# A macaron block on one core: attention without its loop, chunk pairs merged onto the front chunk, keys in twelve pieces, values in quarters

## The chip, the cores and the metric

The kernel runs on one core of one Trainium2 chip, as one program. The metric is the device time in microseconds, and less is better. The engines are named as in the profile: PE (TensorE, matmuls), PEld (its weight loads), DVE (VectorE), ACT (ScalarE), POOL (GpSimd) and SP (SyncE, which here only issues DMAs).

## The reference, cut to what matters

```
x = x + 0.5 * ffn(layernorm(x))          # routed FFN: 128 picked tokens of 1024
x = x + attn(layernorm(x))               # the part that is changed
x = x + 0.5 * ffn(layernorm(x))

# attn: x is (8, 2048, 256): 8 batches, 2048 tokens, 8 heads of 32
q, k, v = lowrank(xh, Uq, Vq, bq), lowrank(xh, Uk, Vk, bk), lowrank(xh, Uv, Vv, bv)
scores = einsum('bqhd,bkhd->bhqk', q, k) / 32 ** 0.5
out = einsum('bhqk,bkhd->bqhd', softmax(scores), v)
```

All of it is float32. The attention takes in for every batch and head a matrix of 2048 x 2048 probabilities.

## The kernel before, in words

The stages follow one another: the first FFN, `project` (q, k and v into HBM as `qk_parts` and `v_tokens`), `attend`, the second FFN. Only `attend` is changed. It has five instruction streams, one for each engine, which are written out by hand and meet in semaphores.

**Units.** A batch has two groups of four heads (`g`), and a group four blocks of 512 queries (`u`), so it has 8 units `un` = 0 to 7, and the stage has 64. A unit has 16 chunks `c` of 128 keys. A chunk gives four tiles, one a head: PE computes the scores into one of three PSUM banks of `at_ps_s` (L1774), ACT takes their exponentials into `at_probs` (L1653), and PE multiplies them by the values into `at_ps_acc` (L1721, `pv`, signalled as `pv_done`). A cycle of a unit is one chunk: four scores, the `pv` of the chunk before, and four matmuls into `at_ps_max` (L1687), by which PE is working out the row maxima of a later unit; DVE reduces these (L1538, L1540) and ACT copies a part (L1602). The maxima reach the queries over a small DMA pair on SP (`row_of_max`, L1408), for which PE waits at the start of each unit (`max_in`, L1791).

**The softmax sums.** `at_probs` is a ring of 8 chunks: chunk c + 8 of the stream reuses the slot of chunk c. POOL sums the chunks 0 to 13 into `at_pool_sum`, in seven additions of 128x2048 (L1516), which I number 0 to 6. It gets help: for the six pairs (2,3), (4,5) ... (12,13) of `DMA_PAIRS` an accumulating DMA of 1 MB, issued by POOL (L1493, `start_pair`), adds one chunk onto the other, and I number these 0 to 5. Addition n, for n over 0, waits until transfer n - 1 has landed. Transfers 0 and 1 are issued ahead of addition 1, and transfer n ahead of addition n from there on (`DMA_BEFORE_ADD`). Chunks 14 and 15 are summed by PE. In cycle 5 of the next unit PE closes the sums (`close_z`, L1732 and L1736), for which it waits for addition 6. Before the exponentials of a chunk ACT waits in `free(c)` for whoever still reads its slot: POOL's addition, the transfer, or the close.

**Loads.** SP issues in each unit, in this order: eight loads of queries for the unit three ahead; a piece of the next group's keys or values; the store of the unit before's result (L1417, once DVE has it); another piece; the `row_of_max` pair, once ACT has the row; in some units a third piece. Keys are loaded in the units with u = 0 to 2 and values (`load_v`, L1392, two halves of 512 KB) in those with u = 3. At the start of each unit with u = 0 PE waits for the values of its group (L1790). All of SP's loads and stores go through one queue, POOL's transfers through another.

**The loop.** Batches 0 and 7 are written out, and 1 to 6 are a loop of three passes of two batches on each engine.

Of the kernel before, what the change touches and what calls it, by code (L numbers as in the profile page):

```python
# [15 lines left out]
P = 128  # L16
# [4 lines left out]
ALU = mybir.AluOpType  # L21
# [3 lines left out]
B, S, D = 8, 2048, 256  # L25
T = S // P
H, DH = 8, 32
HG = P // DH
NG = H // HG
# [1206 lines left out]
DMA_PAIRS = ((2, 3), (4, 5), (6, 7), (8, 9), (10, 11), (12, 13))  # L1236
DMA_BEFORE_ADD = (1, 1, 2, 3, 4, 5)
POOL_CHUNKS = (0, 1, 3, 5, 7, 9, 11, 13)
CLOSE_IN = 5
NORM_IN = 6  # L1240
TURN_MAX_IN = 13
RINGS = 3


def score_banks(tiles, per_cyc):

    users = [w for j in range(tiles) for w in ((j, "m") if j == TURN_MAX_IN * per_cyc + 1 else (j,))]
    order, last, laps = list(range(RINGS)), {}, []  # L1250
    for lap in range(3):
        bank, after = {}, {}
        for w in users:
            if w == CLOSE_IN * per_cyc + 2:
                after["z"] = last.get(RINGS - 1)
                last[RINGS - 1] = ("z", lap)
                order = [1, 0]
            if w == (NORM_IN + 1) * per_cyc + 2:
                order.insert(1, RINGS - 1)
            k = order.pop(0)  # L1260
            order.append(k)
            bank[w], after[w], last[k] = k, last.get(k), (w, lap)
        laps.append((bank, {w: (x[0], lap - x[1]) for w, x in after.items() if x}))
    assert laps[1] == laps[2] and laps[0][0] == laps[1][0]
    return laps[1]


def attend(nc, tag, qk, v_dram, out):

    UQ = 512  # L1270
    NU = S // UQ
# [10 lines left out]
    K_LO_ROWS = ((2 * DH, 0, 2), (DH, 2, 4))  # L1282
    LOADS = 8 * 16
    RING = 8
    NQB = 4
    PER_CYC = TILES // NCYC
    SCALE = float(DH) ** -0.5

    dma_sources = [a for a, _ in DMA_PAIRS]
    pool_chunks = list(POOL_CHUNKS)  # L1290
# [9 lines left out]
    with ExitStack() as ctx:  # L1300
# [67 lines left out]
        def _(sp):  # L1368
# [14 lines left out]

            K_PIECES = [(part, *piece) for part, rows in ((0, HI_ROWS), (0, Q_LO_ROWS), (1, K_LO_ROWS)) for piece in rows]

# [5 lines left out]

            def load_v(b, g, half):  # L1392
                first = half * NC // 2
                sp.dma_start(v[:, g, first:first + NC // 2],
                             v_dram[bass.ds(b * S + first * P, S // 2), g * P:(g + 1) * P]
                             .rearrange("(c p) d -> p c d", p=P)).then_inc(v_in[g], 16)

            def load_kv(b, g):
                load_k(b, g, K_PIECES)
                load_v(b, g, 0)  # L1400
                load_v(b, g, 1)

# [24 lines left out]
            def batch(b, first_batch=False, last=False):  # L1427

                for un in range(BU):
                    unit = b * BU + un  # L1430
                    if un + 3 < BU or not last:

                        sp.wait_ge(scores, unit * TILES)
                        sp.sem_inc(load_turn, 1)
                        load_q(b + (un + 3) // BU, (un + 3) % BU)
                    ahead = not first_batch if un < NU else not last
                    to_load = (b if un < NU else b + 1, 1 if un < NU else 0)
                    u = un % NU
                    if u == 0 and ahead:

                        sp.wait_ge(pv_done, unit * NC)
                        sp.sem_inc(load_turn, 1)
                    if u < NU - 1 and ahead:
                        load_k(*to_load, K_PIECES[3 * u:3 * u + 1])
                    elif ahead:
                        load_v(*to_load, 0)
                    if un > 0:
                        store(unit - 1, b, un - 1)
                    elif not first_batch:
                        store(unit - 1, b - 1, BU - 1)  # L1450
                    if u < NU - 1 and ahead:
                        load_k(*to_load, K_PIECES[3 * u + 1:3 * u + 2])
                    elif ahead:
                        load_v(*to_load, 1)
                    if un + 1 < BU or not last:
                        row_of_max(unit + 1, un + 1)
                    if u < NU - 2 and ahead:
                        load_k(*to_load, K_PIECES[3 * u + 2:3 * u + 3])
                if last:
                    store(b * BU + BU - 1, b, BU - 1)  # L1460

            batch(0, first_batch=True)
            with sp.Fori(0, B // 2 - 1) as pair:
                batch(pair * 2 + 1)
                batch(pair * 2 + 2)
            batch(B - 1, last=True)
# [5 lines left out]
        def _(pool):  # L1472
# [11 lines left out]
            def batch(b, first_batch=False):  # L1484
                for un in range(BU):
# [3 lines left out]
                    def start_pair(d):  # L1489
                        a, c = DMA_PAIRS[d]  # L1490
                        pool.wait_ge(pv_done, unit * NC + c + 1)
                        pool.sem_inc(dma_turn, 1)
                        nc.gpsimd.dma_start(probs[:, c % RING], probs[:, a % RING], accum_op=ALU.add  # L1493
                                            ).then_inc(dma_added[(un * ND + d) % 2], 16)

                    for n in range(ADDS):
# [3 lines left out]
                        c = pool_chunks[n + 1]  # L1500
                        paired = [d for d in range(ND) if DMA_PAIRS[d][1] == c]
                        if paired:
# [15 lines left out]
            batch(0, first_batch=True)  # L1518
            with pool.Fori(0, B // 2 - 1) as pair:
                batch(pair * 2 + 1)  # L1520
                batch(pair * 2 + 2)
            batch(B - 1)
# [3 lines left out]
        def _(dve):  # L1526
# [61 lines left out]
            batch(0, first_batch=True)  # L1588
            with dve.Fori(0, B // 2 - 1) as pair:
                batch(pair * 2 + 1)  # L1590
                batch(pair * 2 + 2)
            batch(B - 1, last=True)
# [3 lines left out]
        def _(act):  # L1596
# [72 lines left out]
            batch(0, first_batch=True)  # L1669
            with act.Fori(0, B // 2 - 1) as pair:  # L1670
                batch(pair * 2 + 1)
                batch(pair * 2 + 2)
            batch(B - 1, last=True)
# [3 lines left out]
        def _(pe):  # L1677
# [18 lines left out]
            pe.wait_ge(q_in[0], LOADS)  # L1696
            pe.wait_ge(k_in[0], LOADS)
            for n in range(FOURS):
# [9 lines left out]
            def batch(b, first_batch=False, last=False):  # L1708
                for un in range(BU):
# [67 lines left out]
                    def max_four(n):  # L1777
# [5 lines left out]
                        if n == 0:  # L1783
                            pe.wait_ge(q_in[ahead % NQB], (b * (BU // NQB) + ahead // NQB + 1) * LOADS)
                            if ahead % NU == 0:
                                pe.wait_ge(k_in[ahead // NU % NG], (b + ahead // BU + 1) * LOADS)
# [34 lines left out]
            batch(0, first_batch=True)  # L1821
            with pe.Fori(0, B // 2 - 1) as pair:
                batch(pair * 2 + 1)
                batch(pair * 2 + 2)
            batch(B - 1, last=True)
# [57 lines left out]
```

## Time and the profile before

| | |
|---|---|
| median of 3 runs | 4640.27 us (4639.2 to 4641.36) |
| profiled execution, its own time | 4629.35 us |
| its span | 4627.6 us |
| granted TensorE clock, mean | 0.929 |
| share of the span busy | PE 81%, DVE 71%, ACT 69%, POOL 55% |

The profiled execution is 10.92 us under the median of the timed runs. A span is the time from the first to the last instruction. Idle time of an engine is put down to what released it, so that `<-POOL at_pool_sum L1516` reads as a wait that ended when that addition ended.

### The profile page before, as it was taken

How to read it: one execution, taken by the hardware profiler on the slowest of the kernel's cores; microseconds unless marked ns; L12 is line 12 of the kernel's file. 1: busy time of each engine (PE TensorE's matmuls, PEld its weight loads, DVE VectorE, ACT ScalarE, POOL GpSimd, SP SyncE). 2: the span in 40 equal slices, each digit the busy share in tenths (PEclk: the TensorE clock that was granted, in tenths of full speed). 3: DMA queues.
4: the chain of work that ended last, by engine and by line, in shares of the span. 5: the costliest groups of instructions: out<-in, count | busy, mean ns of one | idle time of the engine just before them, and what ended most of it. 6: DMA issues, size and time to landing. Idle time of an engine off the chain costs nothing. (4 is left out here: it accounts for less than half of the span.)

```text
span 4627.6 us, 72033 instructions
## 1 busy us (share of the span) xinstructions
PE 3742.8 (81%) x21202; PEld 1462.9 (32%) x21202; DVE 3268.7 (71%) x4504; ACT 3216.1 (69%) x6587; POOL 2553.0 (55%) x966
## 2 busy tenths in 40 slices
PE   0176576599999999999999999999999999930276
PEld 0143354133333333333333333333333333310143
DVE  8644465777777877777777777778777777648544
ACT  5143365488888888878888887888888888834043
POOL 0011000377777777776777777677767777754111
PEclk9988788699999999999999999999999999965588
DMA  8200599677878878777887888788787877678100
GB/s 273 74 5 5 208 344 336 138 146 167 175 160 170 177 158 178 168 168 157 169 169 162 177 169 169 155 169 176 156 178 167 169 165 167 130 214 305 43 5 5
DMA packets 326047, 743.31 MB, mean 161 GB/s; under 512 B 26060, under 2 KB 209888, under 8 KB 270112
## 3 DMA queue, kind: packets, MB, share of 16 engines
q0 software_dynamic: 57216, 407.92, 44.3%
q1 hardware_dynamic: 234880, 297.04, 21.6%
q10 hardware_dynamic: 33568, 33.69, 2.1%
q8 instruction: 185, 3.03, 0.3%
q14 instruction: 198, 1.62, 0.1%
HBM read 198.90 MB, written 136.48 MB: 72 GB/s over the span
## 5 line engine op out<-in xcount | busy, mean ns | idle before, releaser
L1653 ACT ACTIVATE at_probs<-at_ps_s 128x512 f32<-128x512 f32 x4096 | 2255.7, 613 | 346.1 <-PE at_ps_s L1774 261.1
L1538 DVE TENSOR_REDUCE at_part_max<-at_ps_max 128x3 f32<-128x1536 f32 x1024 | 1801.0, 1759 | 472.3 <-PE at_ps_max L1687 464.2
L1516 POOL TENSOR_TENSOR at_pool_sum<-at_pool_sum,at_probs 128x2048 f32<-128x2048 f32 x384 | 1771.9, 4614 | 624.4 <-DMA at_probs<-at_probs 623.4
L1774 PE MATMUL at_ps_s<-at_qs,at_ks 97*128 97x512 f32 (+1 forms) x4096 | 1532.9, 452 | 41.2 <-ACT at_probs L1653 21.4
L1721 PE MATMUL at_ps_acc<-at_probs,at_v 128*32 128x512 f32 x8192 | 1097.5, 608 | 0.9 <-ACT at_probs L1653 0.9
L1774 PEld LDWEIGHTS at_ps_s<-at_qs,at_ks 97*128 97x128 f32 (+1 forms) x4096 | 629.8, 188 | 1151.2 <-ACT at_probs L1653 823.5
L1540 DVE TENSOR_REDUCE at_part_max<-at_max_copy 128x1 f32<-128x512 f32 x1024 | 691.6, 675 | 0.0
L1602 ACT COPY at_max_copy<-at_ps_max 128x512 f32<-128x512 f32 x1024 | 610.0, 596 | 88.1 <-PE at_ps_max L1687 87.6
L1687 PE MATMUL at_ps_max<-at_ks,at_qs 32*128 32x512 f32 x4096 | 525.9, 501 | 68.5 <-DMA at_ks<-qk_parts 34.8
L1493 POOL DMA_DIRECT2D at_probs<-at_probs x384 | 346.1, 901 | 220.6 <-PE at_ps_acc L1721 213.6
L1687 PEld LDWEIGHTS at_ps_max<-at_ks,at_qs 32*128 32x128 f32 x4096 | 198.1, 183 | 425.3 <-issue 363.9
L1516 POOL TENSOR_TENSOR at_pool_sum<-at_probs 128x2048 f32<-128x2048 f32 x64 | 292.1, 4563 | 63.2 <-ACT at_probs L1653 63.2
L1721 PEld LDWEIGHTS at_ps_acc<-at_probs,at_v 128*32 128x32 f32 x8192 | 161.4, 108 | 347.4 <-ACT at_probs L1653 296.0
L1553 DVE RECIPROCAL at_rz<-at_ps_s 128x16 f32<-128x16 f32 x64 | 16.5, 258 | 330.0 <-PE at_ps_s L1743 330.0
L278 PE MATMUL s_pt<-s_ident,s_sall 128*128 128x128 f32 x2 | 0.9, 446 | 271.4 <-DVE s_sall L222 271.4
L1473 POOL MEMSET at_ones<- 128x128 f32 x1 | 0.2, 206 | 333.4 <-POOLq L62 333.4
L259 ACT ACTIVATE s_y<-s_x,s_small 128x256 f32<-128x256 f32 x256 | 129.2, 587 | 68.7 <-DVE s_small L213 61.3
L1732 PE MATMUL at_ps_s<-at_probs,at_ones 128*32 128x512 f32 x1024 | 126.7, 613 | 44.7 <-ACT at_probs L1653 44.7
L1213 PE MATMUL pr_pqk<-pr_xT,pr_w 128*128 128x512 f32 x256 | 132.7, 667 | 32.5 <-DVE pr_lo L1116 29.7
L1646 ACT COPY at_zT<-at_ps_s 128x512 f32<-128x512 f32 x64 | 37.6, 587 | 171.6 <-PE at_ps_s L1736 171.6
L624 POOL TENSOR_TENSOR f_att<-f_att,f_rowsum 128x1280 f32<-128x1280 f32 x16 | 49.6, 3097 | 182.3 <-DVE f_rowsum L709 182.3
L772 ACT ACTIVATE f_small<-f_small 128x4 f32<-128x4 f32 x4 | 0.8, 204 | 207.0 <-DVE f_small L671 207.0
(195 smaller groups left out, 2723.4 us busy)
## 6 DMA issues: line engine op xcount, KB each, us to landing
at_probs<-at_probs POOLq DMA_DIRECT2D x384, 1024.0 KB, 8.3
qk_parts<-pr_hi SPq DMA_DIRECT2D x32, 1024.0 KB, 6.4
qk_parts<-pr_lo SPq DMA_DIRECT2D x32, 1024.0 KB, 6.1
at_qs<-qk_parts SPq DMA_DIRECT2D x320, 64.0 KB, 6.0
at_ks<-qk_parts SPq DMA_DIRECT2D x80, 256.0 KB
s_x<-in_x SPq DMA_DIRECT2D x16, 1024.0 KB, 8.6
after_ffn<-s_y ACTq DMA_DIRECT2D x16, 1024.0 KB, 6.5
pr_x<-after_ffn SPq DMA_DIRECT2D x8, 2048.0 KB
```

The lines of the kernel that those rows point to most:

```text
L259: last = nc.scalar.activation(yb[:, k, t, :], xb[:, k, t, :], ACT.Identity, scale=sm[:, k, 0, t:t + 1], bias=sm[:, k, 1, t:t + 1])
L1213: nc.tensor.matmul(pqk[:, m, :], w[:, m // NG, m % NG, :], xT[:, n % 2, m % NG, :], start=True, stop=True).then_inc(qk_done, 1)
L1493: nc.gpsimd.dma_start(probs[:, c % RING], probs[:, a % RING], accum_op=ALU.add).then_inc(dma_added[(un * ND + d) % 2], 16)
L1516: nc.gpsimd.tensor_tensor(acc, a, probs[:, c % RING], ALU.add).then_inc(pool_added, 1)
L1538: nc.vector.reduce_max(part_max[:, 0:HG - 1, t, c], ps_max[:, 0:HG - 1], AX.X).then_inc(three_max_done, 1)
L1540: nc.vector.reduce_max(part_max[:, HG - 1:HG, t, c], max_copy[:, n % 2:n % 2 + 1], AX.X).then_inc(part_max_done, 1)
L1602: nc.scalar.copy(max_copy[:, n % 2], ps_max[:, HG - 1]).then_inc(max_copied, 1)
L1653: nc.scalar.activation(probs[:, c % RING, h], ps_s[:, BANK[j]], ACT.Exp, scale=SCALE).then_inc(exp_done, 1)
L1687: last = nc.tensor.matmul(ps_max[:, h], qs[rows, un % NQB, h, t * P:(t + 1) * P], ks[rows, un % BU // NU, h, c * 512:(c + 1) * 512], start ...
L1721: last = nc.tensor.matmul(ps_acc[h * DH:(h + 1) * DH, :], v[:, k // NU, c, h * DH:(h + 1) * DH], probs[:, c % RING, h], start=(c == 0), st ...
L1732: nc.tensor.matmul(ps_close[h * DH:(h + 1) * DH, :], ones[:, 0:DH], probs[:, c % RING, h], start=(c == RAW_CHUNKS[0]), stop=False)
L1774: nc.tensor.matmul(ps_s[:, BANK[j]], ks[rows, g, h, c * P:(c + 1) * P], qs[rows, un % NQB, h, :], start=True, stop=True).then_inc(scores, 1)
```

## The change

Six edits, all in `attend`:

1. On all five engines the loop over pairs of batches is replaced by batches 1 to 6 written out.
2. The merge goes the other way: chunk c is added onto chunk a of a pair (a, c), where a was added onto c. A transfer now waits for `pv_done` of a and the exponentials of c, where it waited for `pv_done` of c. POOL's additions take the even chunks 2, 4 ... 12, where they took 3, 5 ... 13. So the even slots come free with an addition and the odd ones with a transfer.
3. Keys come in 12 pieces of one head and 256 KB, where they came in 8 of one to three heads. By u they are placed as 1 + 2 + 1, 1 + 2 + 1 and 1 + 3 pieces (ahead of the store, behind it, behind `row_of_max`); they were 1 + 1 + 1 of one head, then two of one head and one of three, and then two of two heads.
4. Values come in quarters of 256 KB, placed 1 + 2 + 1 in the unit with u = 3, where the halves were placed 1 + 1 + 0.
5. The banks of `at_ps_s` go round as 0, 2, 1, where they went 0, 1, 2. With it the close follows tile 19 in its bank, where it followed tile 20, and tile 30 is the one that waits for the normalised result, where tile 31 was.
6. The counts that PE waits for are changed accordingly.

```diff
-POOL_CHUNKS = (0, 1, 3, 5, 7, 9, 11, 13)
+POOL_CHUNKS = (0, 1, 2, 4, 6, 8, 10, 12)
...
-    order, last, laps = list(range(RINGS)), {}, []
+    order, last, laps = [0, 2, 1], {}, []
...
-                order = [1, 0]
+                order.remove(RINGS - 1)
             if w == (NORM_IN + 1) * per_cyc + 2:
-                order.insert(1, RINGS - 1)
+                order.insert(0, RINGS - 1)
...
-    dma_sources = [a for a, _ in DMA_PAIRS]
+    dma_sources = [c for _, c in DMA_PAIRS]
...
-            K_PIECES = [(part, *piece) for part, rows in ((0, HI_ROWS), (0, Q_LO_ROWS), (1, K_LO_ROWS)) for piece in rows]
+            K_PIECES = [(part, to, h, h + 1) for part, rows in ((0, HI_ROWS), (0, Q_LO_ROWS), (1, K_LO_ROWS))
+                        for to, first, end in rows for h in range(first, end)]
...
-            def load_v(b, g, half):
-                first = half * NC // 2
-                sp.dma_start(v[:, g, first:first + NC // 2],
-                             v_dram[bass.ds(b * S + first * P, S // 2), g * P:(g + 1) * P]
-                             .rearrange("(c p) d -> p c d", p=P)).then_inc(v_in[g], 16)
+            def load_v(b, g, quarters):
+                for q in quarters:
+                    first = q * NC // 4
+                    sp.dma_start(v[:, g, first:first + NC // 4],
+                                 v_dram[bass.ds(b * S + first * P, S // 4), g * P:(g + 1) * P]
+                                 .rearrange("(c p) d -> p c d", p=P)).then_inc(v_in[g], 16)
...
                     if u < NU - 1 and ahead:
-                        load_k(*to_load, K_PIECES[3 * u:3 * u + 1])
+                        load_k(*to_load, K_PIECES[4 * u:4 * u + 1])
                     elif ahead:
-                        load_v(*to_load, 0)
+                        load_v(*to_load, (0,))
                     if un > 0:
                         store(unit - 1, b, un - 1)
                     elif not first_batch:
                         store(unit - 1, b - 1, BU - 1)
                     if u < NU - 1 and ahead:
-                        load_k(*to_load, K_PIECES[3 * u + 1:3 * u + 2])
+                        load_k(*to_load, K_PIECES[4 * u + 1:4 * u + (4 if u == NU - 2 else 3)])
                     elif ahead:
-                        load_v(*to_load, 1)
+                        load_v(*to_load, (1, 2))
                     if un + 1 < BU or not last:
                         row_of_max(unit + 1, un + 1)
                     if u < NU - 2 and ahead:
-                        load_k(*to_load, K_PIECES[3 * u + 2:3 * u + 3])
+                        load_k(*to_load, K_PIECES[4 * u + 3:4 * u + 4])
+                    elif u == NU - 1 and ahead:
+                        load_v(*to_load, (3,))
...
-            with sp.Fori(0, B // 2 - 1) as pair:
-                batch(pair * 2 + 1)
-                batch(pair * 2 + 2)
+            for b in range(1, B - 1):
+                batch(b)
...
                         a, c = DMA_PAIRS[d]
-                        pool.wait_ge(pv_done, unit * NC + c + 1)
+                        pool.wait_ge(pv_done, unit * NC + a + 1)
+                        pool.wait_ge(exp_done, unit * TILES + c * HG + HG)
                         pool.sem_inc(dma_turn, 1)
-                        nc.gpsimd.dma_start(probs[:, c % RING], probs[:, a % RING], accum_op=ALU.add
+                        nc.gpsimd.dma_start(probs[:, a % RING], probs[:, c % RING], accum_op=ALU.add
...
                     if u == 0:
-                        pe.wait_ge(v_in[g], b * 32 + 32)
+                        pe.wait_ge(v_in[g], b * 64 + 64)
                     pe.wait_ge(max_in, unit * 32 + 32)
```

Below is SP's stream in the last unit of batch 0 (un = 7, u = 3), in which the values for the next batch's first group are loaded; `at_v` is the value tile, `attention` the store, `at_max_row` the `row_of_max` pair. First of before, then of the change:

```order
L1378 DMA at_qs<-qk_parts 32x3x512
L1381 DMA at_qs<-qk_parts 32x2x512 x2
L1394 DMA at_v<-v_tokens 128x8x128
L1417 DMA attention<-at_o 128x4x128
L1394 DMA at_v<-v_tokens 128x8x128
L1408 DMA at_qs<-at_max_row 1x12x128
L1408 DMA at_qs<-at_max_row 1x4x128
```

```order
L1379 DMA at_qs<-qk_parts 32x3x512
L1382 DMA at_qs<-qk_parts 32x2x512 x2
L1397 DMA at_v<-v_tokens 128x4x128
L1419 DMA attention<-at_o 128x4x128
L1397 DMA at_v<-v_tokens 128x4x128 x2
L1410 DMA at_qs<-at_max_row 1x12x128
L1410 DMA at_qs<-at_max_row 1x4x128
L1397 DMA at_v<-v_tokens 128x4x128
```

The last quarter of the values now stands behind the `row_of_max` pair; before, nothing but the next unit's queries did.

The second place is the unit ahead of it on SP (un = 6, u = 2), in which the last keys are loaded. First of before, then of the change:

```order
L1389 DMA at_ks<-qk_parts 32x2x2048
L1417 DMA attention<-at_o 128x4x128
L1389 DMA at_ks<-qk_parts 32x2x2048
L1408 DMA at_qs<-at_max_row 1x12x128
L1408 DMA at_qs<-at_max_row 1x4x128
```

```order
L1391 DMA at_ks<-qk_parts 32x2048
L1419 DMA attention<-at_o 128x4x128
L1391 DMA at_ks<-qk_parts 32x2048 x3
L1410 DMA at_qs<-at_max_row 1x12x128
L1410 DMA at_qs<-at_max_row 1x4x128
```

One head moved from ahead of the store to behind it. The third place is the end of the loop's body on PE, before:

```order
L1774 MATMUL at_ps_s<-at_qs,at_ks 128x512
L1683 REGISTER_ALU
L1687 MATMUL at_ps_max<-at_ks,at_qs 128x512 x4
L1822 REGISTER_ALU
L1822 COMPARE_AND_BRANCH
L1774 MATMUL at_ps_s<-at_qs,at_ks 128x512 x2
```

In the change the end of a batch is as the end of any unit:

```order
L1775 MATMUL at_ps_s<-at_qs,at_ks 128x512 x2
L1688 MATMUL at_ps_max<-at_ks,at_qs 128x512 x4
L1775 MATMUL at_ps_s<-at_qs,at_ks 128x512 x2
L1722 MATMUL at_ps_acc<-at_probs,at_v 32x512 x4
```

The branch and the register instructions are gone.

## Rows read from the trace of the kernel before

**Rows 1.** The page, costliest group: count, busy, mean ns, idle before, releaser.

```profile
L1653 ACT ACTIVATE at_probs<-at_ps_s 128x512 f32<-128x512 f32 x4096 | 2255.7, 613 | 346.1 <-PE at_ps_s L1774 261.1
```

**Rows 2.** ACT's first copy of each unit, a window a row: count, starts.

```profile
L1640 ACT COPY at_oT<-at_ps_acc x60: 586/629/632, 1021.5 to 3987.0; 128x512 f32<-128x512 f32 x60
L1640 ACT COPY at_oT<-at_ps_acc x16: 596/629/630, 1266.8 to 2016.1; 128x512 f32<-128x512 f32 x16
L1640 ACT COPY at_oT<-at_ps_acc x2: 629/630/630, 1518.3 to 1566.7; 128x512 f32<-128x512 f32 x2
L1640 ACT COPY at_oT<-at_ps_acc x2: 629/629/629, 1466.0 to 1518.3; 128x512 f32<-128x512 f32 x2
L1640 ACT COPY at_oT<-at_ps_acc x5: 586/587/629, 2016.1 to 2224.4; 128x512 f32<-128x512 f32 x5
L1640 ACT COPY at_oT<-at_ps_acc x4: 586/608/629, 2826.8 to 2983.0; 128x512 f32<-128x512 f32 x4
```

**Rows 3.** Waits from 1000 to 4000 us: total, times, longest.

```profile
POOL at_pool_sum L1516 <- DMA at_probs<-at_probs: 601.6, 294, 6.0
...
ACT at_probs L1653 <- POOL at_pool_sum L1516: 72.9, 63, 2.4
...
PE at_ps_s L1774 <- DMA at_qs<-at_max_row: 3.2, 4, 1.5
```

**Rows 4.** POOL's timeline over one unit: start, length, engine, line, idle before.

```profile
1575.81 4.58 POOL L1516 TENSOR_TENSOR at_pool_sum<-at_pool_sum,at_probs 128x2048 f32<-128x2048 f32 x1 [1.59 <-DMA at_probs<-at_probs]
1580.34 4.56 POOL L1516 TENSOR_TENSOR at_pool_sum<-at_probs 128x2048 f32<-128x2048 f32 x1
1584.85 0.88 POOL L1493 DMA_DIRECT2D at_probs<-at_probs  x1
1588.01 0.86 POOL L1493 DMA_DIRECT2D at_probs<-at_probs  x1 [2.28 <-PE at_ps_acc L1721]
1592.08 4.58 POOL L1516 TENSOR_TENSOR at_pool_sum<-at_pool_sum,at_probs 128x2048 f32<-128x2048 f32 x1 [3.21 <-DMA at_probs<-at_probs]
...
1626.08 4.57 POOL L1516 TENSOR_TENSOR at_pool_sum<-at_pool_sum,at_probs 128x2048 f32<-128x2048 f32 x1 [3.18 <-DMA at_probs<-at_probs]
```

**Rows 5.** ACT's timeline in the same unit, where addition 6 ends.

```profile
1580.51 1.09 ACT L1653 ACTIVATE at_probs<-at_ps_s 128x512 f32<-128x512 f32 x2 [0.62 <-POOL at_pool_sum L1516]
```

**Rows 6.** PE's timeline at the two ends of the loop's body.

```profile
2072.09 1.22 PE L1774 MATMUL at_ps_s<-at_qs,at_ks 97*128 97x512 f32 x2 [7.05 <-issue]
...
2882.20 1.21 PE L1774 MATMUL at_ps_s<-at_qs,at_ks 97*128 97x512 f32 x2 [6.99 <-issue]
```

**Rows 7.** PE's timeline; windows over it: busy, granted clock, DMA share, GB/s.

```profile
1481.90 2.66 PE L1732 MATMUL at_ps_s<-at_probs,at_ones 128*32 128x512 f32 x16 [2.06 <-ACT at_probs L1653]
...
1480.00:1483.00 3.00, 1.10 (x12) 0.42 (x16) 0.59 (x1) 1.08 (x2) 3.00 (x2) 0.99 0.00 0
1483.00:1486.00 3.00, 3.00 (x16) 0.43 (x8) 0.00 (x0) 0.00 (x0) 3.00 (x2) 0.50 0.00 0
```

**Rows 8.** SP's timeline with u = 3; PE's as the next unit starts.

```profile
1439.73 1.14 SPq L1394 DMA_DIRECT2D at_v<-v_tokens  x1
1457.83 1.44 SPq L1408 DMA_DIRECT2D at_qs<-at_max_row  x2
...
1464.15 0.73 PE L1774 MATMUL at_ps_s<-at_qs,at_ks 97*128 97x512 f32 x2
```

**Rows 9.** Store (L1417), issue to landing: whole run, 1000 to 4000, 940 to 1150.

```profile
DMA to landing us min/median/max: 2.3/9.6/11.2
...
DMA to landing us min/median/max: 5.5/9.7/11.2
...
DMA to landing us min/median/max: 7.0/7.5/8.8
```

**Rows 10.** Value halves (L1394), issue to landing, from 1000 to 4000 us.

```profile
DMA to landing us min/median/max: 5.8/9.5/11.8
```

**Rows 11.** POOL's transfers (L1493), issue to landing, from 1000 to 4000 us.

```profile
DMA to landing us min/median/max: 6.9/8.5/12.9
```

More of the change, by code:

```diff
@@ L1283, in attend @@
     LOADS = 8 * 16
+    K_LOADS = 12 * 16
     RING = 8
@@ L1390, in load_k @@
                                  ).then_inc(k_in[g], 16)
-            def load_v(b, g, half):
-                first = half * NC // 2
-                sp.dma_start(v[:, g, first:first + NC // 2],
-                             v_dram[bass.ds(b * S + first * P, S // 2), g * P:(g + 1) * P]
-                             .rearrange("(c p) d -> p c d", p=P)).then_inc(v_in[g], 16)
+            def load_v(b, g, quarters):
[4 more added lines that the diff above has]
+                                 .rearrange("(c p) d -> p c d", p=P)).then_inc(v_in[g], 16)
             def load_kv(b, g):
                 load_k(b, g, K_PIECES)
-                load_v(b, g, 0)
-                load_v(b, g, 1)
+                load_v(b, g, range(4))
             def row_of_max(unit, un):
@@ L1500, in batch @@
                         c = pool_chunks[n + 1]
-                        paired = [d for d in range(ND) if DMA_PAIRS[d][1] == c]
+                        paired = [d for d in range(ND) if DMA_PAIRS[d][0] == c]
                         if paired:
@@ L1518, in _ @@
             batch(0, first_batch=True)
-            with pool.Fori(0, B // 2 - 1) as pair:
-                batch(pair * 2 + 1)
-                batch(pair * 2 + 2)
+            for b in range(1, B - 1):
+                batch(b)
             batch(B - 1)
@@ L1588, in _ @@
             batch(0, first_batch=True)
-            with dve.Fori(0, B // 2 - 1) as pair:
-                batch(pair * 2 + 1)
-                batch(pair * 2 + 2)
+            for b in range(1, B - 1):
+                batch(b)
             batch(B - 1, last=True)
@@ L1669, in _ @@
             batch(0, first_batch=True)
-            with act.Fori(0, B // 2 - 1) as pair:
-                batch(pair * 2 + 1)
-                batch(pair * 2 + 2)
+            for b in range(1, B - 1):
+                batch(b)
             batch(B - 1, last=True)
@@ L1696, in _ @@
             pe.wait_ge(q_in[0], LOADS)
-            pe.wait_ge(k_in[0], LOADS)
+            pe.wait_ge(k_in[0], K_LOADS)
             for n in range(FOURS):
@@ L1785, in max_four @@
                             if ahead % NU == 0:
-                                pe.wait_ge(k_in[ahead // NU % NG], (b + ahead // BU + 1) * LOADS)
+                                pe.wait_ge(k_in[ahead // NU % NG], (b + ahead // BU + 1) * K_LOADS)
                         scores_for_max(unit + ahead - un, ahead, n)
                     if u == 0:
-                        pe.wait_ge(v_in[g], b * 32 + 32)
+                        pe.wait_ge(v_in[g], b * 64 + 64)
                     pe.wait_ge(max_in, unit * 32 + 32)
@@ L1821, in _ @@
             batch(0, first_batch=True)
-            with pe.Fori(0, B // 2 - 1) as pair:
-                batch(pair * 2 + 1)
-                batch(pair * 2 + 2)
+            for b in range(1, B - 1):
+                batch(b)
             batch(B - 1, last=True)
```

## The prediction

> **What bounds the kernel now.** I went from the page to the attention stage, then to one unit of it, then to its exceptions. The page [rows 1] gives the costliest group: ACT's 4096 exponentials, 2255.7 us, with 346.1 us of idle time before them, 261.1 of it ended by PE's scores. To see who ends the waits I took the length of units from ACT's first copy in each [rows 2]. All 59 intervals from 1021.5 to 3987.0 give 50.26 us a unit; the 15 within a pass of the loop give 749.3 / 15 = 49.95. But a unit that nothing disturbs takes 1566.7 - 1518.3 = 48.4 us. So some 1.55 us a unit are waits, and the waits [rows 3] name one that falls on ACT itself: 72.9 us for `at_pool_sum`, in 63 pieces, 1.2 us a unit.
>
> POOL's timeline [rows 4] shows why. Addition 6 of one unit ends at 1575.81 + 4.58 = 1580.39 and that of the next at 1626.08 + 4.57 = 1630.65: a round of 50.3 us. POOL never waits in it for new probabilities at the start; it goes straight on to the next unit's addition 0. It is a chain: addition, transfer, addition, and so on with 10 us of waiting for transfers in a unit (601.6 / 60, [rows 3]). At 1580.51 ACT has waited 0.62 us for exactly that addition 6, which frees the slot of chunk 13 [rows 5]. So two rounds run side by side, ACT and PE at 48.4 us and POOL with its transfers at about 50, and the slower one sets the pace through the ring. POOL's is the slower one while loads are under way.
>
> Three exceptions matter. At each of the two returns to the top of the loop PE stands for 7.05 and 6.99 us, released by nothing but its own issue [rows 6]. A wait of 2.06 us on PE was followed by a granted clock of 0.50 of full speed (1.2 GHz) for a window of 3 us, with 0.99 before it [rows 7]. That unit took 1518.3 - 1466.0 = 52.3 us [rows 2]: 3.9 over the undisturbed one, of which some 2.4 are waits of ACT and 1.5 the slower matmuls. And PE's matmuls waited for the `row_of_max` pair only four times [rows 3]: it lands just in time.
>
> **The change, part by part.**
>
> *The loop.* The four units around the first return take 2224.4 - 2016.1 = 208.3 us, the three around the second 2983.0 - 2826.8 = 156.2 [rows 2]. At 49.95 us a unit they would take 199.8 and 149.9, so the returns cost 8.5 + 6.3 = 14.8 us. Nothing in the written-out batches 0 and 7 shows such a stop, and their register instructions were hidden (the undisturbed unit lies inside the loop and the units are no shorter outside). I take all of it: **-14.8 us**. Bounds: the two stops alone, -14.0; nothing, if the long text stops PE elsewhere.
>
> *The last quarter of the values.* In a unit with u = 3 SP now has a DMA of 256 KB behind the `row_of_max` pair. In the row the pair's issue ends at 1457.83 + 1.44 = 1459.27, and the next unit's first score starts at 1464.15 [rows 8], 4.9 us later. That score stands behind PE's wait for all the values of the group (L1790), so everything on PE is queued behind it, and ACT, DVE and SP's next loads behind PE. Before, the last half went out at 1439.73 [rows 8], 24 us ahead. How long does a quarter take? The nearest row is the store: also 256 KB, also lines of 512 bytes, and it too runs beside POOL's transfers: 9.6 us in the median, 7.0 to 8.8 early on, where few or no keys are loaded, 5.5 at least in the loaded stage, and 2.3 for the last one of the stage, with nothing beside it [rows 9]. The value halves, twice the size, take 5.8 to 11.8 [rows 10]. At this place transfer 4 or 5 is always on its way, as one takes 8.5 us [rows 11] and there are six in 50. I take 9.6, nearest in size, kind and company: a wait of 9.6 - 4.9 = 4.7 us, and 1.5 for the clock behind it [rows 2, 7]. It comes once a group, 14 times (the first two groups are loaded ahead of the stage): 87 us. Some of it comes back: POOL goes on meanwhile, so the next two units should be spared their 1.55 us, as the wait pulls POOL ahead; 14 x 2 x 1.55 = 43 us. Net **+44 us**. Bounds: no wait where the quarter lands in under 4.9 us (0); a wait of 2.1 (landing in 7.0) with the clock, 14 x (3.6 - 3.1) = +7; all unrecovered, +87.
>
> The Trainium skill ("DMA: Bandwidth & Descriptors", section "Anatomy of one DMA — SWDGE (gpsimd) path") puts a DMA at about 2.0 us plus its bytes at 436 GB/s, which for this quarter would be an estimated 2.6 us and no wait at all. No row here shows that with a transfer of POOL beside it; the 2.3 us of the lone store agrees with it.
>
> *The merge.* A transfer may start about one cycle sooner, 48.4 / 16 = 3 us, since it waits for exponentials and not for the later `pv`. But only transfer 1 is held back by `pv` at all (2.28 us at 1588.01 [rows 4]), and addition 1 behind it waits 3.21 us more for transfer 0. Transfers go through one queue, so number 1 starts moving when number 0 is through, whenever it was issued. Against it, addition 6 now frees the slot of chunk 12, which ACT needs one chunk ahead of that of 13: about 3 us less room, taken once, as POOL then runs that much earlier against ACT in every unit. The length of POOL's round stays: **0**. Bounds: -1.55 us in 52 loaded units = -80, if the earlier start did take the waits off ACT; +3 us once, or +1 a unit (+52) if transfers meet the loads worse.
>
> *The keys.* The bytes are the same, 3 MB over three units. The piece of three heads behind `row_of_max` is gone, which spares transfers 4 and 5; more stands behind the store, beside transfers 1 and 2. Transfers range from 6.9 to 12.9 us [rows 11], and no row tells by which load. The waits show none of PE for keys within the stage, and the same bytes are issued in the same unit; **0**, bounds +-1 us in 14 groups. The other quarters have 20 us to land: 0. The turned banks: the close needs tile 19, not 20, and tile 30 the normalised result; both are ready by then. 0, and at most 0.5 us a unit either way. The five more issues of SP in a batch's half lie in its idle time.
>
> Sum: -14.8 + 44 = **+29 us**. The profiled execution's 4629.35 becomes 4659; on the median of 4640.27, 10.92 above it, I expect **4670 us**.
>
> **Rivals.** 0.2% (9 us) is about what a measurement of this kernel can tell.
> - *The forecast*, 0.50: quarters late, half recovered. 4670, from 4635 to 4710.
> - *The quarter lands in time*, 0.12. For it: the lone store, and the page's rule above. Against it: no store or half in the loaded stage landed under 5.5 [rows 9, 10]. Then the returns alone are left: 4640.3 - 14.8 = 4625. It decides where landings fall under 4.9 us.
> - *The front merge frees POOL*, 0.18. For it: after a wait POOL is ahead, and then transfer 1, held by `pv`, starts the chain; exponentials release it sooner. All waits for POOL go (-80), but the 87 us of the quarters come whole, as there is nothing to give back: 4640.3 - 14.8 - 80 + 87 = 4633. It decides once less than 0.15 us a unit of the 1.55 is left.
> - *Both of these*, 0.05: 4640.3 - 14.8 - 80 = 4546.
> - *Nothing comes back*, 0.15: the three us less room eat what the waits give POOL, and the `row_of_max` pair, which lands just in time, comes late as well: 4640.3 - 14.8 + 87 = 4713, and more with the pair.
>
> **From these the numbers.** The range of 4598 to 4732 leaves out the fourth case and the tails of the third and fifth, under 2 in 10. Slower by over 9 us: nearly all of the first (0.45), the fifth (0.15), a quarter of the third (0.05): 0.65. Faster: most of the second (0.10), nearly half of the third (0.08), the fourth (0.05): 0.23. Within: 0.12.
>
> **What the changed profile would show.** PE's timeline free of the two 7 us stops. The first score of 14 units, every fourth, behind an idle of 4 to 5 us released by the DMA of `at_v`, and a window at half clock behind it; landings of the quarters near 9.6 us. ACT's total wait for `at_pool_sum` about half of 72.9 us, now at chunks 2 and 4; undisturbed units still 48.4. If there is no wait on `at_v`, the forecast is wrong in its main step; if the waits for POOL are gone altogether, or as high as before, in what comes back.

## The result and the profile after

The changed kernel takes 4662.26 us (median of 6 runs, 4649.32 to 4675.63) against 4639.46 us for the kernel before (6 runs, 4634.95 to 4641.36, timed beside it). The ratio is 1.0051, 95% interval [1.0035, 1.0067]: some 24 us slower. The forecast was 4670, slower. Its sum of +29 us is near, but partly by luck: the loop written out gives 37 us and not 15, and the keys and the banks, booked at nothing, cost 26 when tried one at a time. These errors cancel.

The profiled execution took 4649.32 us, at the fast end of the six runs and 13 us under their median. So its waits tell where the time goes, not all of it. First the page of the changed kernel (span, then busy time by engine), and the group that answers to [rows 1]:

```profile
span 4647.5 us, 61579 instructions
...
PE 3758.0 (81%) x21202; PEld 1471.5 (32%) x21202; DVE 3266.4 (70%) x4504; ACT 3218.8 (69%) x6587; POOL 2558.9 (55%) x966
...
L1655 ACT ACTIVATE at_probs<-at_ps_s 128x512 f32<-128x512 f32 x4096 | 2252.3, 613 | 358.2 <-PE at_ps_s L1775 307.5
```

The exponentials cost what they did; their idle time grew from 346.1 to 358.2 us, and the part that PE ends from 261.1 to 307.5. The waits of 1000 to 4000 us, which answer to [rows 3] (total, times, longest), say what PE itself waited for:

```profile
POOL at_pool_sum L1520 <- DMA at_probs<-at_probs: 495.3, 252, 5.3
...
ACT at_probs L1655 <- PE at_ps_s L1775: 281.2, 783, 4.2
...
POOL at_probs L1497 <- ACT at_probs L1655: 199.7, 55, 7.3
...
ACT at_probs L1655 <- POOL at_pool_sum L1520: 42.5, 39, 2.8
...
PE at_ps_s L1775 <- DMA at_v<-v_tokens: 37.0, 14, 4.2
...
PE at_ps_s L1775 <- DMA at_qs<-at_max_row: 20.6, 20, 1.8
```

Four things differ from [rows 3]. PE has a new wait for `at_v`, in 14 units as forecast, but of 37.0 / 14 = 2.6 us and not 4.7. Its wait for the `row_of_max` pair has gone from 3.2 us in 4 pieces to 20.6 in 20. ACT's wait for `at_pool_sum` has fallen from 72.9 to 42.5. And POOL waits less for its transfers to land (495.3, where it was 601.6) and more at the start of a transfer: 199.7 us for exponentials (L1497), and 80.5 more that the profile puts to its own issue. In the kernel before its wait there was for `pv`:

```profile
POOL at_probs L1493 <- PE at_ps_acc L1721: 180.9, 65, 7.9
```

So POOL more often stands ready before ACT has anything for it; below this is called time in hand. PE has no wait released by its own issue in this stretch; the two stops of 7 us [rows 6] are gone.

One late quarter, in SP's timeline (start, length, engine, line), with the answer for that one DMA alone:

```profile
2275.73 2.09 SPq L1410 DMA_DIRECT2D at_qs<-at_max_row  x2
2277.86 1.24 SPq L1397 DMA_DIRECT2D at_v<-v_tokens  x1
...
DMA to landing us min/median/max: 7.4/7.4/7.4
```

and in PE's timeline of the same kernel, followed by windows over that place (length, busy times, granted clock, DMA share, GB/s):

```profile
2281.62 0.51 PE L1688 MATMUL at_ps_max<-at_ks,at_qs 32*128 32x512 f32 x4
2285.35 1.22 PE L1775 MATMUL at_ps_s<-at_qs,at_ks 97*128 97x512 f32 x2 [3.22 <-DMA at_v<-v_tokens]
...
2280.90:2284.40 3.50, 1.23 (x10) 0.49 (x6) 3.10 (x4) 1.95 (x4) 1.77 (x2) 1.00 1.08 222
2284.40:2294.60 10.20, 9.25 (x32) 2.88 (x32) 2.47 (x3) 4.93 (x10) 7.02 (x2) 0.50 0.69 170
```

The quarter goes out at 2277.86 and lands 7.4 us later, at 2285.3, and the first score starts then. The row tells the price too: after an idle of 3.22 us the granted clock is 0.50 (1.2 GHz) for 10.2 us, where [rows 7] had 3 us of it after a wait of 2.06. The pair of scores takes 1.22 us there and 0.73 in [rows 8]. Such a stretch stands behind 9 of the 14 waits for `at_v`.

### The profile page after: what moved, and what is told of

Read it like the earlier page. It is cut to its first block and busy times, and to the rows that moved or that the text cites. A ratio compares the mean times of both kernels' runs of the same rounds, so it can differ in the third digit from the quotient of the medians.

```text
span 4647.5 us, 61579 instructions
## 1 busy us (share of the span) xinstructions
PE 3758.0 (81%) x21202; PEld 1471.5 (32%) x21202; DVE 3266.4 (70%) x4504; ACT 3218.8 (69%) x6587; POOL 2558.9 (55%) x966
## 5 line engine op out<-in xcount | busy, mean ns | idle before, releaser
L1655 ACT ACTIVATE at_probs<-at_ps_s 128x512 f32<-128x512 f32 x4096 | 2252.3, 613 | 358.2 <-PE at_ps_s L1775 307.5
L1775 PE MATMUL at_ps_s<-at_qs,at_ks 97*128 97x512 f32 (+1 forms) x4096 | 1548.7, 456 | 88.4 <-DMA at_v<-v_tokens 37.0
L1722 PE MATMUL at_ps_acc<-at_probs,at_v 128*32 128x512 f32 x8192 | 1111.9, 615 | 0.9 <-ACT at_probs L1655 0.9
L1497 POOL DMA_DIRECT2D at_probs<-at_probs x384 | 350.8, 914 | 323.7 <-ACT at_probs L1655 227.6
L805 ACT ACTIVATE f_att<-f_att,f_rowmax 128x128 f32<-128x128 f32 x256 | 98.7, 388 | 47.5 <-DVE f_rowmax L705 47.5
```

The source lines that it names most:

```text
L805: last = nc.scalar.activation(att[:, s, h], att[:, s, h], ACT.Exp, scale=ATT_SCALE, bias=rowmax[:, s, h:h + 1], accum_out=rowsum[:, s, h:h ...
L1497: nc.gpsimd.dma_start(probs[:, a % RING], probs[:, c % RING], accum_op=ALU.add).then_inc(dma_added[(un * ND + d) % 2], 16)
L1655: nc.scalar.activation(probs[:, c % RING, h], ps_s[:, BANK[j]], ACT.Exp, scale=SCALE).then_inc(exp_done, 1)
L1722: last = nc.tensor.matmul(ps_acc[h * DH:(h + 1) * DH, :], v[:, k // NU, c, h * DH:(h + 1) * DH], probs[:, c % RING, h], start=(c == 0), st ...
L1775: nc.tensor.matmul(ps_s[:, BANK[j]], ks[rows, g, h, c * P:(c + 1) * P], qs[rows, un % NQB, h, :], start=True, stop=True).then_inc(scores, 1)
```

## Experiments

Each was timed in 5 rounds (one in 3) beside the kernel before. The ratio is to the kernel before in the same comparison; its difference from 1, times 4640 us, is the "cost" below. Medians of the kernel before were 4641.08 (first four experiments), 4638.0 (next four) and 4636.93 (last four).

**The loop written out, and nothing else.** Only the five loops change:

```diff
-            with pe.Fori(0, B // 2 - 1) as pair:
-                batch(pair * 2 + 1)
-                batch(pair * 2 + 2)
+            for b in range(1, B - 1):
+                batch(b)
```

> The kernel before with batches 1 to 6 written out on all engines, and nothing else. My theory: the two stops of 7 us are gone and nothing takes their place, 4640 - 15 = 4625. Rival (POOL used the stops to catch up, and its waits on ACT come instead): 4635 to 4640, with ACT's wait for at_pool_sum up from 73 to 85 us or more.

4604.44 us (4602.93 to 4609.81, 5 runs), ratio 0.992 [0.9907, 0.9933]: -37 us, two and a half times the term of the sum.

**Quarters alone**: the kernel before with the values in quarters, the last one behind `row_of_max`.

```diff
-                        load_v(*to_load, 1)
+                        load_v(*to_load, (1, 2))
...
+                    elif u == NU - 1 and ahead:
+                        load_v(*to_load, (3,))
```

> The kernel before with the values in quarters, placed 1 + 2 + 1, and nothing else. My theory: PE waits for at_v in 14 units; by the forecast's sum +44 us (4684), by the wait that the changed kernel shows (2.6 us, not 4.7) 14 x (2.6 + 1.5 - 3.1) = +14 us (4654). Rival (POOL gives it all back): 4640. Transfers stand about 3 us later here than in the changed kernel, so the quarter may meet another one and land at another time.

4651.52 us (4644.86 to 4660.21, 11 runs), ratio 1.0017 [1.0008, 1.0027]: +8 us. Its waits from 1000 to 4000 us:

```profile
PE at_ps_s L1776 <- DMA at_v<-v_tokens: 8.3, 2, 4.1
```

Two waits in place of the 14 of the changed kernel, from the same order on the queue. So the place in the order alone does not make the quarter late.

**The front merge alone.**

```diff
-POOL_CHUNKS = (0, 1, 3, 5, 7, 9, 11, 13)
+POOL_CHUNKS = (0, 1, 2, 4, 6, 8, 10, 12)
...
-                        pool.wait_ge(pv_done, unit * NC + c + 1)
+                        pool.wait_ge(pv_done, unit * NC + a + 1)
+                        pool.wait_ge(exp_done, unit * TILES + c * HG + HG)
```

> The kernel before with the pairs merged onto the front chunk, and nothing else. My theory: 0, 4635 to 4643, ACT's wait for at_pool_sum unchanged at about 73 us but at chunks 2 and 4. Rival of the forecast (the front merge frees POOL): up to -80 us, 4560 to 4620, with that wait near 0. Rival: the three us less room make it worse, 4645 to 4690, with more waits for at_pool_sum or for at_max_row.

4636.07 us (4613.39 to 4648.71, 12 runs), ratio 0.9987 [0.9973, 1.0001]: -6 us, not told from zero. The merge does in part what the third rival said: its waits show POOL held up by exponentials (245.4 us), and 53.0 us of ACT's waiting for POOL, less than the 72.9 of [rows 3] but far from gone:

```profile
ACT at_probs L1654 <- POOL at_pool_sum L1517: 53.0, 36, 4.0
...
PE at_ps_s L1775 <- DMA at_qs<-at_max_row: 12.7, 22, 1.8
```

**The changed kernel with its last quarter issued early**, in one go with the two ahead of `row_of_max`:

```diff
-                        load_v(*to_load, (1, 2))
+                        load_v(*to_load, (1, 2, 3))
...
-                    elif u == NU - 1 and ahead:
-                        load_v(*to_load, (3,))
```

> The changed kernel, but with the last quarter of the values issued with the second and third, ahead of the row_of_max pair. My theory: the wait of PE for at_v at 14 units (37 us in the changed kernel's profile) and the low clock behind it are gone, POOL's wait on ACT grows again by some, net 44 us less than the changed kernel: 4662 - 44 = 4618, below the kernel before by about 20. Rival (the pace is POOL's, and what a wait of PE costs POOL gives back in full): 4650 to 4665, with ACT's wait for at_pool_sum back at 70 us or more. Rival (the late row_of_max pair is the cost): 4655 or so, with PE's waits for at_max_row unchanged at 20 to 28 us.

4630.44 us (4627.8 to 4633.6, 8 runs), ratio 0.9974 [0.9964, 0.9984]. The wait for `at_v` is gone, and the place of the quarter costs 1.0051 - 0.9974, or 36 us, in the changed kernel, where 44 had been expected. The late `row_of_max` pair stays (18.7 us of waits in 17), and ACT waits as long for POOL as in the kernel before:

```profile
ACT at_probs L1653 <- POOL at_pool_sum L1518: 72.8, 59, 3.2
```

With the quarter late it is 42.5 us. So the waits of PE do let POOL get ahead, and some 30 us come back.

**One batch a pass, so five returns in place of two**, in all five engines:

```diff
-            with pe.Fori(0, B // 2 - 1) as pair:
-                batch(pair * 2 + 1)
-                batch(pair * 2 + 2)
+            with pe.Fori(0, B - 2) as i:
+                batch(i + 1)
```

> The kernel before with the loop's body cut to one batch: six passes, five returns to the top instead of two. Written out it was 36.7 us faster, not 15. My theory (each return costs a fixed amount, the stop of PE and what follows it): if it is 18 us a return, 4641 + 3 x 18 = 4696; if it is the 7.4 us of the forecast, 4663. Rival (what costs is that waits and addresses come from registers, wherever the returns are): 4641, as the registers stay.

4665.85 us (4663.08 to 4671.93, 4 runs, 3 rounds), ratio 1.0058 [1.0044, 1.0073]: +27 us for three more returns, 9 each, not far from the 7.4 of the forecast. The five returns against none are 27 + 37 = 64 us, or 12.8 each; the forecast had 7.4. PE's waits from 1000 to 4000 us show 6 by its own issue. Five are the returns, of 4.1 to 7.2 us; the sixth is one of 0.7 us at 1071 us, far from any return:

```profile
PE at_ps_s L1770 <- issue: 30.0, 6, 7.2
```

**Twelve pieces of keys, and nothing else.**

```diff
-            K_PIECES = [(part, *piece) for part, rows in ((0, HI_ROWS), (0, Q_LO_ROWS), (1, K_LO_ROWS)) for piece in rows]
+            K_PIECES = [(part, to, h, h + 1) for part, rows in ((0, HI_ROWS), (0, Q_LO_ROWS), (1, K_LO_ROWS))
+                        for to, first, end in rows for h in range(first, end)]
```

> The kernel before with the keys in 12 single-head pieces, nothing else. My theory: 0, 4636 to 4646. Rival (the three-head piece behind row_of_max is the worst neighbour of a transfer, so it helps): 4620 or less, with ACT's waits for at_pool_sum down. Rival (more behind the store holds up transfers 1 and 2): 4650 or more.

4657.77 us (4641.71 to 4663.96, 7 runs), ratio 1.004 [1.0026, 1.0055]: +19 us where the sum had nothing, as the rival had it. In its waits PE doesn't wait for keys, and ACT waits more for POOL than the 72.9 of [rows 3]:

```profile
ACT at_probs L1655 <- POOL at_pool_sum L1518: 91.0, 72, 2.2
```

**The order of the banks alone.**

```diff
-    order, last, laps = list(range(RINGS)), {}, []
+    order, last, laps = [0, 2, 1], {}, []
...
-                order = [1, 0]
+                order.remove(RINGS - 1)
...
-                order.insert(1, RINGS - 1)
+                order.insert(0, RINGS - 1)
```

> The kernel before with the banks going round as 0, 2, 1, nothing else. My theory: 0, 4636 to 4646, undisturbed units at 48.4 us. Rival: up to half a microsecond a unit, 4670, with undisturbed units longer.

4650.82 us (4632.9 to 4656.71, 11 runs), ratio 1.0016 [1.0005, 1.0027]: +7 us, small but told from zero. In its waits PE stands 13.8 us for the `row_of_max` pair, in 12 pieces (3.2 in 4 before), and ACT 83.7 for POOL (72.9 before), so the turned banks do move the streams against each other.

**The changed kernel with the merge turned back** (later chunk as the destination again, with the waits of a transfer as they were; quarters, keys, banks and written-out batches stay):

```diff
-                        nc.gpsimd.dma_start(probs[:, a % RING], probs[:, c % RING], accum_op=ALU.add
+                        nc.gpsimd.dma_start(probs[:, c % RING], probs[:, a % RING], accum_op=ALU.add
```

> The changed kernel with the merge turned back onto the later chunk, all else as changed. v_early showed 26 us over the written-out kernel that the merge, the keys or the banks must hold. If the merge holds them (its earlier phase makes the row_of_max pair late: 20 to 28 us of PE waits in the changed kernel, 2 to 4 without the front merge): 4662 - 25 = 4637, with those waits near 5 us. If the keys or the banks do: 4655 to 4668, with the waits for the pair still there.

4638.52 us (4632.66 to 4646.7, 11 runs), ratio 0.9999 [0.999, 1.0008]: in the changed kernel the merge costs 24 us, though it gains 6 alone. Without it the parts do add: the four that are left come to -37 + 8 + 19 + 7 = -3 us one at a time, and measured together to 0. Its waits from 1000 to 4000 us:

```profile
ACT at_probs L1654 <- POOL at_pool_sum L1519: 133.7, 107, 2.1
...
PE at_ps_s L1774 <- DMA at_v<-v_tokens: 5.3, 3, 3.3
...
PE at_ps_s L1774 <- DMA at_qs<-at_max_row: 2.3, 4, 0.8
```

In these two profiles the merge takes 91 us of waiting for POOL off ACT (133.7 to 42.5) and gives PE 32 us of waiting for `at_v` and 18 for `row_of_max`. Why does it make the quarter late? POOL's timeline of this kernel and the answer for its quarter at 2285.47:

```profile
2278.80 0.88 POOL L1496 DMA_DIRECT2D at_probs<-at_probs  x1
...
2285.47 0.44 SPq L1397 DMA_DIRECT2D at_v<-v_tokens  x1
...
DMA to landing us min/median/max: 3.0/3.0/3.0
```

and the transfer in the changed kernel before the quarter at 2277.86, with its own answer:

```profile
2275.10 0.86 POOL L1497 DMA_DIRECT2D at_probs<-at_probs  x1
...
DMA to landing us min/median/max: 7.9/7.9/7.9
```

In the changed kernel POOL's transfer went out 2.8 us ahead of the quarter and landed at 2283.0, and the quarter landed 2.3 us after it. With the merge turned back the transfer had gone out 6.7 us ahead and was nearly through (it landed 7.4 us after its issue), and the quarter took 3.0 us. The trace gives the landings of 7 last quarters of the changed kernel: 5.5 to 8.8 us after their issue, each behind a transfer begun 1.4 to 3.7 us before; ahead of the other 7 it was begun 0.9 to 1.9 us before. With the merge turned back it gives all 14: eleven behind a transfer begun 5.3 to 7.0 us before, which took 3.0 to 4.7 us, and three behind one begun 1.4 to 4.1 us before, which took 4.1 to 8.2. In all 21 the quarter landed 0.6 to 2.4 us after that transfer. So the quarter's time is what is left of a transfer of POOL's and some 1 to 2 us more, and the merge sets what is left.

The kernel with the quarters alone bears this out. In 12 of its 14 groups the transfer had gone out 5.5 to 9.0 us before the last quarter, and PE did not wait. In the other two (quarters at 1666.03 and 2491.82) it had gone out 0.8 us before, and these are the two units in which PE waited, 4.1 us each.

**Is it these two parts?** If so, merge and quarters in the kernel before, with loop, keys and banks as they were, must be far over the sum of both. The edits are those of the two experiments above.

> The kernel before, loop kept, with two parts of the change: the front merge and the values in quarters with the last one behind the row of maxima. Alone, the merge came to -5 us and the quarters to +10 us. Theory (the merge moves GpSimd's transfers onto the last quarter): the first score of 10 or more of the 14 units waits for at_v, 25 to 40 us in all on TensorE, and the time is 4655 to 4675 us, over the sum of the two parts. Rival (the parts add up): at most 4 such waits, as in the run with the quarters alone, and 4640 to 4648 us.

4668.61 us (4667.05 to 4686.07, 6 runs), ratio 1.0073 [1.0057, 1.0088]: +34 us, where the parts alone add up to +2. The theory holds: 12 waits for `at_v` in place of 2, and in all 14 groups the transfer goes out 0.7 to 3.7 us before the last quarter, which lands 5.0 to 8.1 us after its issue. The kernel's waits from 1000 to 4000 us:

```profile
PE at_ps_s L1777 <- DMA at_v<-v_tokens: 30.8, 12, 3.3
...
PE at_ps_s L1777 <- issue: 11.3, 2, 5.7
...
PE at_ps_s L1777 <- DMA at_qs<-at_max_row: 10.1, 12, 1.8
```

**Written-out batches and the merge**, values in halves.

> The kernel before with the batches written out (4604 us by itself) and the front merge, values in halves. Theory (the merge costs only through the late quarter): 4594 to 4610 us, no wait for at_v. Rival (without the returns the merge costs by itself, through row_of_max arriving late and the clock that falls behind it): 4620 to 4635 us, with TensorE waiting over 20 us for at_max_row.

4589.6 us (4585.33 to 4594.48, 4 runs), ratio 0.9893 [0.9878, 0.9907]: the fastest of all, 50 us under the kernel before by the ratio and 13 under the one that is only written out, a little below what the theory gave. The merge costs nothing where no quarter stands behind it, and it takes ACT's wait for POOL down (59.8 us in the kernel only written out):

```profile
ACT at_probs L1651 <- POOL at_pool_sum L1516: 38.3, 26, 3.2
...
PE at_ps_s L1771 <- DMA at_qs<-at_max_row: 6.6, 10, 1.8
```

**Only PE's loop written out**; the other four engines keep theirs.

> The kernel before with the batches written out on TensorE alone; the other four engines keep their loop of three rounds. Written out on all five it took 4604 us, 37 less than before. Theory (what a return costs is TensorE's own stop of 7 us and what follows from it): 4600 to 4612 us. Rival (the returns of ScalarE, GpSimd and the DMA queue's engine cost too, as the other engines stop at the same point): 4615 to 4635 us, with a wait of TensorE for the exponentials of several us at the two returns.

4633.17 us (4626.88 to 4636.76, 11 runs), ratio 0.9986 [0.9977, 0.9996]: -6 us of the 37. The rival holds. ACT's timeline at the two returns shows what PE's stop had covered:

```profile
2079.15 1.09 ACT L1653 ACTIVATE at_probs<-at_ps_s 128x512 f32<-128x512 f32 x2 [2.35 <-issue]
...
2885.64 1.08 ACT L1653 ACTIVATE at_probs<-at_ps_s 128x512 f32<-128x512 f32 x2 [4.63 <-issue]
```

and PE stands behind it for 4.12 us, in its own timeline:

```profile
2886.29 0.79 PE L1774 MATMUL at_ps_s<-at_qs,at_ks 128*128 128x512 f32 x1 [4.12 <-ACT at_probs L1653]
```

**The changed kernel with the keys in 8 pieces again.**

> The changed kernel with the keys in 8 pieces again (12 in the change); quarters, front merge, banks and the written-out batches stay. Theory (the key pieces cost in the changed kernel what they cost alone, about 20 us): 4636 to 4648 us. Rival (they cost nothing here, since what they put behind the stores is only seen by units that no longer wait for it): 4656 to 4668 us, with the 14 waits for at_v as in the changed kernel.

4634.34 us (4622.69 to 4652.35, 12 runs), ratio 0.9997 [0.9983, 1.0011]: the keys cost 25 us in the changed kernel. The price is the theory's, just over it, though the waits for `at_v` stay as the rival had them; those for `row_of_max` go back to what they were:

```profile
PE at_ps_s L1774 <- DMA at_v<-v_tokens: 32.7, 14, 4.3
...
PE at_ps_s L1774 <- DMA at_qs<-at_max_row: 2.4, 6, 1.2
```

## Why the prediction was right, and where its steps were not

The direction, the place of the main loss and the total held. By what the runs showed the sum is

| part | forecast, us | alone | in company |
|---|---|---|---|
| batches written out | -14.8 | -37 | |
| last quarter late | +44 | +8 | 36 in the changed kernel |
| front merge | 0 | -6 | -13 on the written-out kernel, +24 in the changed one |
| keys in 12 pieces | 0 | +19 | 25 in the changed kernel |
| banks | 0 | +7 | |

Alone, the five parts come to -37 + 8 - 6 + 19 + 7 = -9 us. Measured together they are +24. The difference of 33 is, within what can be told, the merge and the quarter together: 34 - (8 - 6) = 32 us.

Set against the forecast: the loop gave 22 us more than its term, the quarter with the merge cost 34 as a pair where 44 stood for them, and the keys and the banks cost 26 where nothing stood. That is 22 + 10 less and 26 more, so +29 becomes +23. The direction rests on the quarter, which was forecast; that the total came so near is luck.

*The loop: a term mis-sized.* "I take all of it: -14.8 us" read two returns off two stretches of one execution [rows 2]. Written out, the kernel gained 37. One step was missing. The stop of 7 us was taken for PE's own, but the other engines return at the same point: with only PE's loop gone, 6 of the 37 us came, and ACT's own 2.35 and 4.63 us of stop stood in the open. What POOL, DVE and SP lose at a return isn't shown. That still doesn't make 37: the three more returns cost 9 us each, and by that price two are 18. The two profiled executions differ by less than the medians (spans 4627.6 and 4604.0, so 23.6 us), as that of the kernel before lies 11 us under its median. What is left stays open; waits and addresses that come from registers, as they do in both looped kernels and not in the written-out one, were never tried apart from the returns. The Trainium skill ("Runtime: NRT & Kernel Launch", section "Instruction fetch mechanics") says that a taken branch whose target is not among the two instruction pages at hand has to fetch that page first, and calls this an instruction-fetch stall; the stops of PE and ACT that go with the loop agree with it, and the page has no price for one.

*The last quarter: right in size, by other steps.* The 14 waits came where the prediction put them, and its three pieces were there, each smaller than it had them. "I take 9.6" was too long: the seven landings in the trace are 5.5 to 8.8 us, 6.5 in the median, and the waits came to 37 us, not 14 x 4.7 = 66. For the clock it had 14 x 1.5 = 21. From 1000 to 4000 us the clock record has 102 us at half clock in the changed kernel and 65 in the one with its quarter early. A cycle takes 4.9 us at half clock and 2.8 at full clock (last section), so the 37 more cost an estimated 37 x (1 - 2.8 / 4.9) = 16. And of "14 x 2 x 1.55 = 43 us" that come back, 30 did (72.8 to 42.5). That makes 37 + 16 - 30 = 23 us, where the two spans (4647.5 and 4628.8) differ by 18.7; the 36 of the medians is more, since the changed kernel's profile is the fastest of its six executions. Waits too long and a recovery too large cancelled in part.

How much comes back isn't fixed. With the keys in 8 pieces ACT waits 38.8 us for POOL with the late quarter, and 38.3 in the kernel of written-out batches and merge, which has none: nothing came back there, and the two are 1.0% or 48 us apart, the banks included. So "there is nothing to give back", the third rival's line, held in that pair and not in the change. The row behind "9.6" was the store's, all with transfers beside them in whatever phase; the row to ask was how long ahead of the quarter POOL's transfer goes out.

*The merge: the step that failed.* "The length of POOL's round stays: 0" took the queue of transfers for the limit. The wait for `pv` that could be saved was weighed at the 2.28 us of one row; it was 2.8 in the mean of 65 and up to 7.9. Transfers were released sooner all the same: ACT's wait for POOL fell from 133.7 to 42.5 us between the changed kernel with the old merge and with the new one. The prediction had the bounds right (-80 if ACT's waits go, +52 "if transfers meet the loads worse") and took the middle. Both ends happened at once, gain on POOL and loss on the loads, and in the change the loss was the larger by 24 us.

*The keys: a term mis-sized.* "0, bounds +-1 us in 14 groups" was +19 alone and 25 in the change. The bytes and the units are the same, but the loads stand elsewhere in the queue. Alone the price shows as ACT's wait for POOL (91.0 against 72.9, +18); with the merge, where POOL has time in hand, as the `row_of_max` pair (20.6 against 2.4, +18). That the same loads hit whoever has no slack is a reading of these profiles and not shown: the merge alone, with 8 pieces, also has 12.7 us of waits for the pair. Which piece is to blame was not tried.

*Banks.* +7 where "at most 0.5 us a unit" had allowed up to 30. The `row_of_max` pair comes late more often with them (13.8 us of waits against 3.2); by which link was not tried.

*The rival that decided otherwise.* "The quarter lands in time" is not what happens here, but it is what mostly happens in the two kernels without the merge: 2 or 3 waits in place of 14, and landings from 2.8 us, near the 2.3 of the lone store [rows 9], to 4.7 where the transfer ahead was over 5 us old. The trigger it named, landings under 4.9 us, fits them; what decides on them is POOL's phase, that is, how far its transfer has got when the quarter is issued.

*The other signs.* The shortest units still take 48.3 to 48.4 us, and the stops are gone. ACT's wait for POOL is 42.5 us, not far from the half of 72.9 that was named. The stretch at half clock stands behind 9 of the 14 late quarters, for 3 to 14 us.

## What to carry to other kernels

Ask of a late load not how long it takes, but what other transfer it is issued behind and by how many microseconds; here a part of the change that shifted another engine by 4 us added 32 us to an edit that costs 8 alone. Time the parts in pairs where one moves an engine's phase and another puts a load at the edge, for the parts alone add up to the wrong sign. And when a wait of the slowest engine is removed, look for the same stop on the next one, as here on ACT behind PE, before booking a gain.

## What the runs showed of the hardware

A load of 256 KB landed 3.0 us after its issue when POOL's accumulating transfer (1 MB, 7.4 us) had gone out 6.7 us before it, and 7.4 us after when that was 2.8 us before it. In all 21 landings that the traces of these two kernels have, the load landed 0.6 to 2.4 us after the transfer ahead of it, which took 7.4 to 9.6. That the load waits for the bytes of the transfer, and does not share with it evenly, fits them, but no run tests it by itself.

The granted clock fell after waits of PE as short as 1.29 us (the one ahead of 1519.12 in the changed kernel), but not after each longer one: behind waits of 2.50 and 2.66 us, ahead of 3098.14 and 3299.38, it stayed at 1.00. After the 2.89 us ahead of 2076.12 in the changed kernel it was 0.50 (1.2 GHz) for 13.7 us, with 0.99 before and 1.00 after it (windows, columns as above):

```profile
2072.00:2076.20 4.20, 1.31 (x11) 0.57 (x7) 3.22 (x4) 1.95 (x4) 2.65 (x3) 0.99 1.03 209
2076.20:2089.90 13.70, 13.70 (x44) 4.11 (x44) 4.70 (x4) 7.32 (x14) 11.54 (x3) 0.50 0.57 129
2089.90:2094.00 4.10, 4.10 (x27) 1.59 (x30) 3.05 (x3) 3.80 (x8) 0.88 (x1) 1.00 0.00 0
```

PE is busy for all of the 13.7 us at the lower level, and ACT for 7.32 of them, so PE sets the pace there. A cycle takes 4.9 us in it (scores at 2079.13 and 2084.03) and 2.8 at full clock (2275.41 and 2278.19), so these 13.7 us cost an estimated 5.9 more than at full clock, twice the wait ahead of them.

A return of the loop cost more than PE's stop of 4 to 7 us: 9 us for each of three more, and some 18 for each of the two that were removed, if nothing else went with them.
